# Cross-attention chain on one core: the extra key's vector made by TensorE, and the single tile's maxima turned in another bank

## What is computed

```python
h  = layer_norm(x) * scale + offset
qh = (h @ wq + bq).reshape(b, q_len, 16, 128)
kh = (ctx @ wk + bk).reshape(b, 1500, 16, 128)
vh = (ctx @ wv + bv).reshape(b, 1500, 16, 128)
kh = concatenate([kh, bias_k]); vh = concatenate([vh, bias_v])   # one extra key and value per head
weights = softmax(einsum('bqhk,bthk->bhqt', qh, kh) / sqrt(128))
x = x + einsum('bhqt,bthk->bqhk', weights, vh).reshape(b, q_len, 2048) @ wo + bo
```

## Time and profile before

| | us |
|---|---|
| runs shown, median (lowest to highest) | 1891.01 (1883.81 to 1891.54) |
| the profiled execution, its own time | 1889.87 |
| its span, first to last instruction | 1888.1 |
| PE busy | 1685.1 (89%) |
| DVE busy | 1206.0 (64%) |
| ACT busy | 1041.3 (55%) |
| POOL busy | 904.0 (48%) |

### The profile page before, as it was taken

One profiled execution on the slowest core, in us unless ns is written; L12 is line 12 of the kernel. 1 busy time (PEld: TensorE's weight loads), 2 busy tenths in 40 slices (PEclk: granted clock), 3 DMA queues, 4 the chain that ended last, 5 costly groups with the idle time before them and its releaser, 6 DMA issues.

```text
span 1888.1 us, 40609 instructions
## 1 busy us (share of the span) xinstructions
PE 1685.1 (89%) x12516; PEld 1577.2 (84%) x12516; DVE 1206.0 (64%) x2350; ACT 1041.3 (55%) x2021; POOL 904.0 (48%) x688
## 2 busy tenths in 40 slices
PE   3698888987689999999999999789999999999997
PEld 2577777776569999999999987689999999999986
DVE  5577777757385656656656667765665665666664
ACT  2466666656363654655555556445654654655563
POOL 4456655532154444444445448443543552553573
PEclk8899999989799999999999999899999999999998
DMA  7767666656042101111110103321110010010021
GB/s 232 191 158 172 171 168 163 172 127 152 7 118 68 35 32 65 39 35 56 48 50 33 53 18 99 101 83 42 34 62 36 33 65 33 33 65 0 1 81 43
DMA packets 113943, 149.65 MB, mean 79 GB/s; under 512 B 25476, under 2 KB 99716, under 8 KB 113860
## 3 DMA queue, kind: packets, MB, share of 16 engines
q1 hardware_dynamic: 112516, 142.42, 27.2%
q10 hardware_dynamic: 1344, 6.19, 1.0%
HBM read 108.28 MB, written 3.42 MB: 59 GB/s over the span
## 4 chain that ended last, share of the span: by engine, by line
PE 58%; DVE 12%; SPq 10%; issue 7%; POOL 5%; DMA 4%; ACT 3%; DVEq 1%; ACTq 0%; POOLq 0%
PE ps L761 11%; PE ps L763 10%; PE ps L762 10%; PE ps L1008 6%; PE ps L1012 6%; PE ps L1010 6%; SPq L379 6%; DMA q<-q_scratch 2%; SPq L382 2%; POOL rr L713 2%; PE ps L975 2%; DVE ar L1987 1%; DVE ar L1804 1%; SPq L380 1%; PE ps L988 1%
## 5 line engine op out<-in xcount | busy, mean ns | idle before, releaser
L713 POOL TENSOR_TENSOR rr<-ar,rr 125x512 fp32r<-125x512 f32 x336 | 443.5, 1358 | 443.4 <-ACT rr L1445 258.5
L1008 PE MATMUL ps<-cx,rr 125*128 125x258 f32 x1344 | 399.1, 297 | 0.4
L1012 PE MATMUL ps<-cx,rr 125*128 125x258 f32 x1344 | 381.9, 284 | 0.0
L1010 PE MATMUL ps<-cx,rr 125*128 125x256 f32 x1344 | 381.3, 284 | 0.0
L761 PE MATMUL ps<-rr,ct 128*125 128x256 f32 x1152 | 332.3, 288 | 4.5 <-DVE ar L1845 2.7
L763 PE MATMUL ps<-rr,ct 128*125 128x256 f32 x1152 | 326.5, 283 | 0.0
L762 PE MATMUL ps<-rr,ct 128*125 128x256 f32 x1152 | 326.4, 283 | 0.0
L1432 ACT ACTIVATE ar<-ar 125x512 f32<-125x512 f32 x336 | 208.4, 625 | 110.8 <-DVE ar L1847 62.0
L1008 PEld LDWEIGHTS ps<-cx,rr 125*128 125x128 f32 x1344 | 255.5, 190 | 3.7 <-DVE ar L1835 3.7
L1012 PEld LDWEIGHTS ps<-cx,rr 125*128 125x128 f32 x1344 | 257.0, 191 | 0.0
L1010 PEld LDWEIGHTS ps<-cx,rr 125*128 125x128 f32 x1344 | 256.9, 191 | 0.0
(11 more groups left out here) (202 smaller groups left out, 3744.6 us busy)
## 6 DMA issues: line engine op xcount, KB each, us to landing
raw_t<-in_ctx_t SPq DMA_DIRECT2D x24, 1500.0 KB, 6.6
k<-khl SPq DMA_DIRECT2D x192, 187.5 KB
raw<-in_ctx SPq DMA_DIRECT2D x16, 1500.0 KB
raw<-in_ctx SPq DMA_DIRECT2D x8, 1408.0 KB
raw<-stat_scratch ACTq DMA_DIRECT2D x7, 750.0 KB, 3.9
w_raw<-in_wq SPq DMA_DIRECT2D x32, 128.0 KB, 2.6
w_raw<-in_wk SPq DMA_DIRECT2D x32, 128.0 KB, 2.9
w_raw<-in_wv SPq DMA_DIRECT2D x32, 128.0 KB, 2.3
```

The source lines that it names most:

```text
L713: pool.tensor_tensor(group(p[:, 1, :, :], u, k), x, f(group(p[:, 0, :, :], u, k)), ALU.subtract)\
L1008: pe.matmul(ps[:, bank, 0:D + 2], hi, cx[0:KC, c, 0:D + 2], start=c == 0, stop=False, skip_group_check=True)
L1010: pe.matmul(ps[:, bank, 0:D], hi, cx[0:KC, c, D + 2:CW], start=False, stop=False, skip_group_check=True)
L1012: mm = pe.matmul(ps[:, bank, 0:D + 2], lo, cx[0:KC, c, 0:D + 2], start=False, stop=c == CH - 1, skip_group_check=True)
```

## The change

In the attention the single tile's maxima are turned and spread in bank 5 instead of 7 (with waits for that bank), between other chunks (8 and 12 in place of 6 and 11). `sums` of the tile 0 before it goes ahead of the shift on DVE, behind one of the three context splits, its `scale_output` ahead of the exponentials on ACT, and PE no longer waits for `m_ready` before tile 1. The vector u is made by PE, within `norm`: 32 float32 matmuls of one column a layer, 6 behind the mean, 12 behind the squares, 14 behind the spreading, from a turned copy of wq (16 DMAs of 128 KB a layer, into parts of `qo` that are free then). `key_bias`, `extra_key` of DVE and `whole_h` go, with 32 DMAs a layer; ACT and DVE split u once, and the logits are made with 6 fp32r matmuls. POOL's third low weight part of i = 1 moves from the end of layer 0 to behind the norm. SP loads four more small constants, and takes the turned weights of i = 2 behind head 11's weights in `outputs(1)`.

```diff
+        u_hl = sb("u_hl", [P, 2, DH, H], F32R)
-        N_CONST = 15
+        N_CONST = 19
+        def key_weights(i, h):
+            e, b, at0 = (1, h % B, HPB * TQ * 2 * (h // B)) if i == 1 else (h // B, h % B, 0)
+            at0 = ROWS * b + at0 + 3 * 64
+            return qo[:, e, at0:at0 + D]
+        MAX_BANK = [7 if u < UNITS - 1 else 5 for u in range(UNITS)]
@@ -462,17 +472,13 @@
-                    if kind == "a" and n >= NS:
-                        sp.wait_ge(s["u_ready"], H * (i - 1) + n - NS + 1)
-                    if kind == "o" and n < NS:
-                        sp.wait_ge(s["u_ready"], H * (i - 1) + H + n - NS + 1)
...
-                if kind == "a":
-                    for c, name in enumerate(("biask", "bk")):
-                        row = io[f"{name}{i}"].rearrange("h k -> (h k)")[n * P:(n + 1) * P].partition_broadcast(P)
-                        sp.dma_start(dk_raw[:, slot, c * P:(c + 1) * P], row).then_inc(s[f"dk_in{slot}"], 16)
+            def turned_weights(i):
+                for h in range(H):
+                    sp.dma_start(key_weights(i, h), io[f"wqt{i}"][h * K:(h + 1) * K, :]).then_inc(s["wt_in"], 16)
...
             head_rows(1)
+            sp.wait_ge(s["zs"], GT0)
+            turned_weights(1)
...
                 for n in range(2 * NS - 1, H):
                     step_weights("o", i, n)
+                    if i == 1 and n == H - 5:
+                        sp.wait_ge(s["oh_lo"], B)
+                        turned_weights(2)
@@ -646,9 +652,8 @@
-                if kind == "plain" and t >= 5:
+                if kind == "plain" and t in (5, 6):
                     weight_low("a", 1, t - 5)
-                    key_bias(1, t - 5)
...
                 norm(i - 1)
-                for n in range(NS - 1, H):
-                    key_bias(i, n)
+                if i == 1:
+                    pool.wait_ge(s["h_lo"], DH)
+                for n in range(NS - 1 if i > 1 else NS - 2, H):
                     weight_low("a", i, n)
-                    if n == NS + 1:
-                        whole_h(i - 1, V[f"o{i}"])
@@ -957,6 +953,8 @@
+                    if u == 0 and j == MAX_BANK[UNITS - 1]:
+                        pe.wait_ge(s["m_ready"], n)
...
                 pe.wait_ge(s["run_max"], units(i, b, u) + 1)
-                if o_before is not None:
+                if not pair(u):
+                    pe.wait_ge(s["s_free"], CH // 2 * (units(i, b, u) + 1))
+                elif o_before is not None:
                     pe.wait_ge(s["o_back"], o_before)
+                bank = MAX_BANK[u]
...
+            def extra_key(i, heads):
+                for h in heads:
+                    if h == 0:
+                        pe.wait_ge(s["dk_ready"], 1)
+                        pe.wait_ge(s["wt_in"], 16 * H * i)
+                    for e in range(DH):
+                        mm = pe.matmul(ps[:, 7, H * e + h:H * e + h + 1], key_weights(i, h)[:, e * P:(e + 1) * P],
+                                       kc[:, i - 1, 0, h:h + 1], start=True, stop=True)
+                    if h == H - 1:
+                        mm.then_inc(s["u_made"], 1)
...
+                beside = [range(0, 3), range(3, 9), range(9, H)] if n < 2 else [(), (), ()]
...
-                        pe.wait_ge(s["u_ready"], H * i)
-                        pe.wait_ge(s["ht_ready"], DH * i)
+                        pe.wait_ge(s["u_lo"], i)
                         for e in range(DH):
-                            mm = pe.matmul(ps[0:H, 7, 0:NQ], u_k[:, e, :], ht[:, e, :], start=e == 0, stop=e == DH - 1)
+                            mm = three(pe, ps[0:H, 7, 0:NQ], u_hl[:, 0, e, :], u_hl[:, 1, e, :], hs[:, 0, e, :],
+                                       hs[:, 1, e, :], e == 0, e == DH - 1)
...
-                    first_at, next_at = (6, CH - 1) if not pair(nu) else (4, 9) if pair(u) else (3, 8)
+                    first_at, next_at = (8, CH) if not pair(nu) else (4, 9) if pair(u) else (3, 8)
...
                     if pair(u):
-                        pe.wait_ge(s["m_ready"], units(i, nb, nu) + 1)
+                        if pair(nu):
+                            pe.wait_ge(s["m_ready"], units(i, nb, nu) + 1)
@@ -1506,13 +1525,15 @@
                     extra_prob(i, nb, nu)
+                    if not pair(nu):
+                        scale_output(i, b, u, 0)
                     exponentials(i, nb, nu, 0)
...
-                        if k == 0:
+                        if k == 0 and pair(nu):
                             scale_output(i, b, u, 0)
...
+                    if n == 2:
+                        act.wait_ge(s["u_made"], i)
+                        act.activation(u_hl[:, 0, :, :], ps[:, 7, 0:DH * H].rearrange("p (e h) -> p e h", e=DH),
+                                       ACT.Copy).then_inc(s["u_hi"], 1)
@@ -1686,6 +1711,9 @@
+            dve.wait_ge(s["const_dma"], 16 * N_CONST)
+            dve.tensor_tensor(kc[:, :, 0, :], kc[:, :, 0, :], kc[:, :, 1, :], ALU.subtract).then_inc(s["dk_ready"], 1)
...
+                    def next_context(j):
+                        if not last or i == 1:
+                            split_ct(*((i + 1, 0) if last else (i, b + 1)), j)
                     def beside_shift(k):
-                        if not pair(nu) and (not last or i == 1):
-                            split_ct(*((i + 1, 0) if last else (i, b + 1)), k)
-                        if k == (1 if pair(nu) else 0):
+                        if pair(nu) and k == 1:
                             sums(i, b, u, 0)
+                        if not pair(nu) and k:
+                            next_context(k)
...
                     row_max(i, nb, nu)
+                    if not pair(nu):
+                        next_context(0)
+                        sums(i, b, u, 0)
                     shift(i, nb, nu, beside_shift)
...
-                    for m in {0: (1,), 1: (2, 3), 2: (4, 5)}.get(n, (n + 3,) if n + 3 < H else ()):
-                        extra_key(i, m)
+                    if n == 4:
+                        split_key(i)
```

More of the change, by code:

```diff
@@ L93, in build @@
         gate_t = sb("gate_t", [P, 2])
+        kc = sb("kc", [P, 2, 2, H])
         hb = sb("hb", [P, 4, H])
@@ L232, in build @@
             "o_ready", "o_t", "o_back",
-            "w_hi", "w_lo", "dk_ready", "u_ready", "oh_hi", "oh_lo", "dv_ready",
+            "w_hi", "w_lo", "dk_ready", "u_made", "u_hi", "u_lo", "oh_hi", "oh_lo", "dv_ready",
             "m1", "h1_hi", "h1_lo", "gelu_done", "m2", "qe_act", "qe_dve",
-            "x_ready", "ln_pe", "ln_dve", "ln_sq", "ln_pow", "h_hi", "h_lo", "ht_ready",
+            "x_ready", "ln_pe", "ln_dve", "ln_sq", "ln_pow", "h_hi", "h_lo",
             "small_dve", "fix_v", "small_pe", "small_dma",
@@ L365, in constants @@
                                   ("bq1", hb[:, 0, :]), ("bv1", hb[:, 1, :]), ("bq2", hb[:, 2, :]),
-                                  ("bv2", hb[:, 3, :])):
+                                  ("bv2", hb[:, 3, :]), ("biaskc1", kc[:, 0, 0, :]), ("bkc1", kc[:, 0, 1, :]),
+                                  ("biaskc2", kc[:, 1, 0, :]), ("bkc2", kc[:, 1, 1, :])):
                     sp.dma_start(dst, io[name]).then_inc(s["const_dma"], 16)
@@ L616, in weight_low @@
                 low(w_s[:, 2 * slot + 1, :], w_raw[:, slot, :], w_s[:, 2 * slot, :]).then_inc(s["w_lo"], 1)
[L618 to L622, removed]
             def slot(b, t, n, kind):
@@ L680, in norm @@
                 pool.tensor_tensor(rs4, rs4, mhalf[0:QC, 0:NQ // QC], ALU.pow).then_inc(s["ln_pow"], 1)
[L682 to L686, removed]
             def extra_value(i, n):
@@ L752, in _ @@
                     weight_low(*NEXT["o", i], n)
-                    if i == 1:
-                        key_bias(2, n)
             norm(2)
@@ L969, in turn_max @@
                 pe.wait_ge(s["run_max"], units(i, b, u) + 1)
-                if o_before is not None:
+                if not pair(u):
+                    pe.wait_ge(s["s_free"], CH // 2 * (units(i, b, u) + 1))
+                elif o_before is not None:
                     pe.wait_ge(s["o_back"], o_before)
+                bank = MAX_BANK[u]
                 for k in range(4):
                     to = 2 * (k % 2) + k // 2 if pair(u) else k
-                    mm = pe.transpose(ps[:, 7, KC * to:KC * (to + 1)], run[0:KC, P * k:P * (k + 1)], ident[0:KC, 0:KC])
+                    mm = pe.transpose(ps[:, bank, KC * to:KC * (to + 1)], run[0:KC, P * k:P * (k + 1)], ident[0:KC, 0:KC])
                 mm.then_inc(s["max_t"], 1)
@@ L1025, in norm @@
                 mm.then_inc(s["ln_pe"], 1)
+                extra_key(n + 1, beside[0])
                 for e in range(DH):
@@ L1031, in norm @@
                     mm.then_inc(s["ln_pe"], 1)
+                extra_key(n + 1, beside[1])
                 pe.wait_ge(s["ln_dve"], LN_V * n + 5)
@@ L1035, in norm @@
                     .then_inc(s["ln_pe"], 1)
+                extra_key(n + 1, beside[2])
```

(20 more changed lines are left out.)

9 lines of the change are left out of this document (3 added, 6 removed).

## The result

The changed kernel takes 1835.9 us (median of 4 runs, 1835.65 to 1838.89) against 1888.58 (4 runs): ratio 0.9727, 95% interval 0.9701 to 0.9753. The forecast was 1831 with a range of 1815 to 1853. The profiled execution took 1835.65 us at a span of 1833.9.

A forecast was written before the change was run, and what follows sets the result against it. The prediction took PE, busy 89% of the span, as the bound, so gains come from its idle time or work. Its terms summed to -59.3 us, from 1889.87 to 1830.6; it said 1831 us, range 1815 to 1853.

The forecast's parts named there:

- The maxima's turning and tile 0's output: Attention: PE's waits for DVE's last maximum and ACT's scaled output go, 0.65 and 2.53 us in each of 14 regular batches.
- Tile 1's output: Attention, one step later: 0.15 us of new PE wait a regular batch, bounds 0 and 1.5 us.
- The first rival: Attention: the output's wait moves to tile 1's output, 1.5 us, through ACT's wait for DVE's reciprocal and DVE's list; 1850 us, chance 0.13.
- The last batches: Attention, last batch of each layer: DVE's 0.9 us of idle is won, with part of PE's wait; -2.2 us for both.
- The clock in the attention: PE's clock no longer drops behind the gap in 5 of 14 regular batches, 1.7 us each: -8.5 us.
- Layer 0's end: PE's wait for POOL's spread goes as a weight part and `key_bias` leave its front: -3.9 us.
- The norms: The 32 one-column products: first 6 free, the rest partly or wholly at low clock, +5.4 us a layer, +10.8 in all.
- The second rival: Norms: the one-column products hold the clock, 6.5 us a layer better; 1818 us, chance 0.13.
- Queries and logits: Work leaving DVE, POOL and SP shortens PE's waits in queries, -10.7 us; fewer-pass logits products, -0.9 us for both layers.
- The DMAs: Turned weights and four small constants cost nothing; those of i = 2 delay head 12's weights with 1 us to spare.
- The third rival: Attention: the single tile's probabilities come too late for PE because scaling stands before the exponentials; 1911 us, chance 0.03.
- The fourth: Rival: early `sums` no earlier in effect and norms cost 16 us; some 1882 us, or no measurable change; chance 0.04.

The follow-up runs named there:

- e9a: Changed kernel with the later maxima's turning in bank 5 kept, but sums and scaling of tile 0 put back where they were: 1892.4 us, ratio 1.0009.
- e9b: Changed kernel with early sums and scaling kept, but the maxima turned in bank 7 behind 6 chunks, with the waits of before: 1847.7 us, ratio 0.9782.
- e10: Changed kernel with POOL's low parts of the single tile's probabilities cut to 16 of 512 columns in two of three groups: 1822.7 us, ratio 0.9647.
- e1: Kernel before with the attention's edits only, u still made on DVE and POOL: 1850.4 us, ratio 0.9806.
- e6: e5 plus 6, 10 and 10 unread products of 448 columns in the three gaps of the first two norms: 1826.1 us, ratio 0.9665.
- e5: Changed kernel with one product of 32 columns in place of a layer's 32 one-column products: 1830.0 us, ratio 0.968.
- e3: Changed kernel with DVE's third split of the next context moved behind the sums of tile 1: 1826.8 us, ratio 0.9673.

## Why the prediction was right, and where it was off

The sum was -59.3 us (its terms add up to -59.2); the profiled execution has -54.2. Term by term:

**The maxima's turning and tile 0's output (0.65 and 2.53 a batch): right.** Neither has a wait left. e9a and e9b show a coupling that the prediction did not: the first saves nothing without the second.

**Tile 1's output: mis-sized.** "I take 0.15 us of new wait; bounds are 0 and 1.5 us"; it is 1.0. The step that failed is "DVE's sums come behind its last split (706.5)", which gave the split the 1.19 us of the earlier trace rows. It had slid to where POOL's operation starts first, and takes 2.29. That is 14 x 0.85 = 12 us; by the period, 66.6 us where 66.0 was forecast, 9 us. The first rival named the place and DVE's list, but not the cause: e10 removes the wait with the reciprocal and the order of DVE's list left as they are.

**The last batches: wrong sign.** I took -2.2 us. In layer 1 the same collision stretches three DVE operations (one before), and PE's gap is 5.33 us from start to start where it was 3.2 in two; behind it the clock is low for 3.4 us, which it was not before. To the last turned output layer 1's last batch is 2.5 us longer and layer 2's 1.4 shorter: +1.1 in all.

**The clock in the attention (-8.5): right.** It stays at 1.00 in the 14 regular batches. The five batches with a fall had a period of 70.5 us against 69.0, so 7.3 us. Regular batches (14 x 2.4 us), clock and last batches make some -40 us, the two stages of the table -39.7; e1 measured -37.8. The sum had -53.1.

**Layer 0's end: too small.** From DVE's reciprocal to the norm it was 21.9 us and is 16.3: -5.6, not -3.9, since the operations that follow the wait now run at the higher clock (L863 takes 0.94 us for four, 1.09 for two). The other 4 us of the -9.6 lie ahead of that reciprocal, and I can't count them as the change's: the nine kernels with the layer 0 of the kernel after (itself among them) have it anywhere between 476.3 and 480.9 us, and e1, with the layer 0 of before, has it 3 us earlier than the kernel before. They hide about a third of the 13 us by which the attention fell short, and that is luck. Without them the sum would have been off by some 9 us, still inside its range.

**The norms (+10.8): right**, +9.8, and by the mechanism given: free at first, then at the low clock. The reason given was weaker than it looked. In the stretch behind 24.2 us in the earlier trace rows PE is idle for all but 0.24 of 2.80 us, so its fall of the clock does not show that the products failed to hold it. The kernel after and e6 do. The norms also vary, 15.1 to 18.1 us in the 14 norms of seven kernels that have them, and with them the moment of the fall: 7.1 us behind the norm's start in the shortest, 3.8 us in the longest. The rule of the Trainium skill, "TensorE: Matmul & The Clock Gate", Part 1, that activity releases the throttle, does not hold for these products, and the measurement decides: the clock was 0.50 with PE busy 3.00 us of 3, as the profile counts it. For products of 448 columns (e6) it does hold. The second rival, 1818 us, falls with it. The -1.4 us for a recovery of the clock in the queries were not found: e5's have the same length.

**Queries and logits (-11.6):** -14.2 in all, all of it ahead of the first product of the scores (51.4 to 43.4 us and 49.0 to 42.8).

**The DMAs (nothing): right, but with no margin left.** The turned weights of i = 2 keep SP for 8.8 us, not the 5.6 of the forecast. ACT's copy of head 12's weights waits 0.57 us for them, and PE doesn't wait.

The third rival never came near: no regular batch has a wait for the single tile's probabilities. The fourth is excluded by the gap at tile 0's output, which is gone, and by norms that cost 10 us in all, not 16.

## What to carry to other kernels

When an edit moves a two-input DVE operation in time, look at what POOL is doing at its new place: its duration in the old place is its price in the new one only if it starts first there as well, and whatever stands behind it pays. Put what another engine waits for in front of such an operation (e3: 9.1 us for one split moved). Filling PE's gaps with one-column products costs nothing while the gap lasts and saves nothing of the clock; price what lies beyond the gap at the low clock.

## What the runs showed of the hardware that was not expected

- A split of 128x1000 on DVE takes 1.19 us alone or started ahead of POOL's subtraction, 2.29 us when started 0.10 us behind it, 1.85 us when started 0.54 us behind it; in both it ends 1.06 us after POOL. Two of 128x448 take 3.28 us instead of 1.17. The profile shows all this as duration, not as a wait, and names no releaser.
- PE at 3.00 us busy of 3 with one-column products reads a clock of 0.50; with 448-column products 1.00. One 448-column product behind every four records of one column does not hold it.
- In the regular batches, idle stretches of PE of 2.4 us ahead of tile 0's output were followed by a fall of the clock in 5 of 14, those of 3.0 us (e9a) in all 14, those of 0.9 us ahead of tile 1's in none.
